# A graph-attention stack on one core: first weighing ahead of the second fold, three adds ahead of the second weighing

## What is computed

```python
for l in range(L):
    xn = _layernorm(h, ln1_g[l], ln1_b[l])
    q = (xn @ wq[l] + bq[l]).reshape(n, H, DH)
    k = (xn @ wk[l] + bk[l]).reshape(n, H, DH)
    v = (xn @ wv[l] + bv[l]).reshape(n, H, DH)
    scores = jnp.einsum('ehd,ehd->eh', q[dst], k[src]) * scale
    m = jax.ops.segment_max(scores, dst, num_segments=n)
    ex = jnp.exp(scores - m[dst])
    z = jax.ops.segment_sum(ex, dst, num_segments=n)
    attn = ex / z[dst]
    agg = jax.ops.segment_sum(attn[:, :, None] * v[src], dst, num_segments=n)
    ...
```

## Time and profile before

| | |
|---|---|
| median of 3 runs | 6146.24 us (6140.39 to 6148.77) |
| the profiled execution, its own time | 6137.13 us |
| its span, from first to last instruction | 6135.2 us |
| mean granted TensorE clock over the span | 0.759 of 2.4 GHz |
| DVE busy over the span | 3292.3 us (54%) |
| POOL busy | 3409.4 us (56%) |
| PE busy | 3529.9 us (58%) |
| first attention pass | about 3084 to 3783 us of the span |
| second attention pass | about 4181 to 4897 us |

### The profile page before, as it was taken

How to read it: one execution, slowest core, us unless ns; L and a number is a source line. 1 busy time by engine, 2 the same in 40 slices (tenths; PEclk the granted TensorE clock), 3 DMA queues, 4 the chain that set the end, 5 groups by cost and what they waited for, 6 DMA issues and landing times. The chain is left out here.

```text
span 6135.2 us, 56916 instructions
## 1 busy us (share of the span) xinstructions
PE 3529.9 (58%) x14811; PEld 2769.4 (45%) x14811; DVE 3292.3 (54%) x6546; ACT 1408.6 (23%) x3123; POOL 3409.4 (56%) x3358
## 2 busy tenths in 40 slices
PE   0365237774300067774677775887777667955551
PEld 0265126663100056663455553775555466434441
DVE  7497325555300047767678887347888742122225
ACT  0000112221200022221355553334555332200000
POOL 3778777776788747773066663005666400057771
PEclk9755656775655558876889997998999888977776
DMA  1043134443200034543277775016777610333333
GB/s 42 2 107 75 28 78 130 127 128 51 51 2 2 3 89 132 133 129 68 97 215 201 201 200 135 18 55 198 201 202 200 151 35 22 143 114 100 99 99 49
DMA packets 289802, 630.60 MB, mean 103 GB/s; under 512 B 79692, under 2 KB 134320, under 8 KB 286384
## 3 DMA queue, kind: packets, MB, share of 16 engines
q0 software_dynamic: 168256, 437.11, 29.2%
q1 hardware_dynamic: 121328, 190.89, 9.7%
HBM read 560.35 MB, written 66.48 MB: 102 GB/s over the span
## 5 line engine op out<-in xcount | busy, mean ns | idle before, releaser
L875 PE MATMUL edge_sums<-edge_rows,edge_hot 128*128 128x272 f32 (+3 forms) x4640 | 1575.3, 505 | 767.1 <-issue 285.4
L875 PEld LDWEIGHTS edge_sums<-edge_rows,edge_hot 128*128 128x128 f32 x4640 | 1155.0, 257 | 1087.6 <-issue 369.8
L809 POOL DMA_INDIRECT edge_rows<-kv_rows,dst_index x928 | 877.6, 946 | 1157.7 <-POOLq L89 661.2
L809 POOL DMA_INDIRECT edge_rows<-rel_rows,dst_other_index x464 | 471.0, 1015 | 693.3 <-ACTq L89 552.3
L809 POOL DMA_INDIRECT edge_rows<-xl_rows,dst_index x464 | 465.9, 1004 | 213.6 <-issue 135.2
L809 POOL DMA_INDIRECT edge_rows<-rows,src_index x464 | 462.2, 996 | 156.7 <-issue 131.9
L1141 PE MATMUL edge_own_rows<-dst_x,edge_hot_t 128*128 x1856 | 458.8, 392 | 37.5 <-ACT edge_hot_t L840 21.1
L211 POOL DMA_INDIRECT table_dst<-proj_dst_put_stage x350 | 417.2, 1192 | 98.0 <-issue 86.3
L1141 PEld LDWEIGHTS edge_own_rows<-dst_x,edge_hot_t 128*128 128x128 f32 x1856 | 352.3, 195 | 106.3 <-issue 53.2
L1032 DVE TENSOR_TENSOR edge_rows<-edge_rows,edge_turn_p 128x2048 f32<-128x2048 f32 x174 | 396.6, 2279 | 1.7 <-ACT edge_rows L1250 1.3
L1528 PE MATMUL proj_prod<-proj_w,proj_turned 128*128 128x512 f32 (+1 forms) x900 | 367.2, 554 | 1.0 <-ACT proj_turned L1476 0.9
(11 more groups left out here) (391 smaller groups left out, 5790.3 us busy)
## 6 DMA issues: line engine op xcount, KB each, us to landing
edge_where<-local_dst SPq DMA_DIRECT2D x174, 256.0 KB, 3.4
dst_rank_keys<-in_dst SPq DMA_DIRECT2D x85, 312.5 KB, 3.5
rel_rows<-proj_out SPq DMA_DIRECT2D x25, 1024.0 KB, 3.8
edge_where<-local_src SPq DMA_DIRECT2D x58, 256.0 KB, 3.5
edge_rows<-kv_rows,dst_index POOLq DMA_INDIRECT x928, 3.8
kv_rows<-proj_out SPq DMA_DIRECT2D x50, 260.0 KB, 2.0
edge_rows<-rows,src_index POOLq DMA_INDIRECT x464, 2.9
edge_rows<-xl_rows,dst_index POOLq DMA_INDIRECT x464, 2.9
```

The costliest lines, as they stand in the source:

```text
L809: pool.indirect_dma_start(out=self.rows[:, h * U + b, 0:self.width], out_offset=None, in_=self.source[:, :], in_offset=bass.IndirectOffset ...
L875: last = nc.tensor.matmul(sums[p % len(sums)][:, 0:width], self.hot[s % 2][:, 2 * (p % 4) + i, :], self.half(s)[:, 2 * (p % 4) + i, first: ...
```

## The change

In DVE's `step_dot`, after `multiply(4f + 3)`, the order was second fold, first weighing, fix, second weighing, four adds. It becomes first weighing, fix, second fold, three adds, second weighing, fourth add. No instruction is added or removed; nothing changes on the other engines' lists. The lines below the diff move by three.

```diff
--- before.py
+++ after.py
@@ -1069,15 +1069,18 @@
                     add(8 * d + 7, tiles[3])
                 if chunk(f):
                     multiply(4 * f + 3)
-                    fold(2 * f + 1)
                 if chunk(c):
                     weigh(2 * c)
                     tiles = e.node_tiles(nc, dve, 2 * c)
                     fix(c, tiles[0])
+                if chunk(f):
+                    fold(2 * f + 1)
+                if chunk(c):
+                    dve.wait_ge(fixed, c + 1)
+                    for n in range(3):
+                        add(8 * c + n, tiles[n])
                     weigh(2 * c + 1)
-                    dve.wait_ge(fixed, c + 1)
-                    for n in range(4):
-                        add(8 * c + n, tiles[n])
+                    add(8 * c + 3, tiles[3])
 
             def step_sum(f):
                 c, d = f - 1, f - 2
```

## The result

The changed kernel takes 6126.89 us in the median of 19 runs, the kernel before 6140.39 us in the median of as many taken beside them: a ratio of 0.9978 (95% interval 0.9972 to 0.9985), 13.5 us less. The forecast was 90 us less. Its profiled execution has a span of 6119.7 us.

What follows compares the result with a forecast made beforehand. DVE was taken to set the pace in the attention passes, waiting for slow pairs. Per pass 26 chunks x 1.8 us, less 2; two passes about 90 us, so 6146.2 - 90 = 6056 us, range 6036 to 6110.

Steps and rivals of the forecast that it cites:

- The rule named from the Trainium skill: Rival at PE's pauses: two no better than one, clock falls in each chunk, 6150 us, no change; chance 0.09.
- The end of a pass: Last chunk of each attention pass: no fold covers the pairs, last add at 7.5 instead of 5.9, 2 us lost.

Runs made afterwards that it cites:

- after_fill: The changed kernel with five idle 128x128 matmuls more per chunk on PE, behind the first half's pairs and ahead of the turn; 6052.6 us, ratio 0.986.
- after_swap: The changed kernel with expand(4f+1) put ahead of turn_scores(c) in PE's order; 6036.1 us, ratio 0.9832.
- after_work: The changed kernel with one DVE memset of 128x640 more per chunk, ahead of multiply(4f+2); 6136.9 us, ratio 1.0003.

## Why the prediction was wrong

```profile
2313.82 0.35 PE L1172 MATMUL edge_turn_p<-edge_shape,edge_lead_hot 8*128 8x8 f32 x2 [1.92 <-DVE edge_raised_t L1009]
```

From 2316.35 to 2323.10 the clock was 0.50 there, behind this pause and one of 1.12 us; a hint, if no measure for the attention passes. The runs show that in these passes pauses of 2.5 and 2.3 us ahead of the turn always or nearly always bring a fall right behind them, 2.06 and 1.85 in part of the chunks; right behind the 1.6 ahead of the pairs and the 1.4 ahead of the turn (after_fill) it came in none. The length of one pause doesn't decide it alone: in after_swap the clock fell with none above 0.8 us near, in after_work behind 1.50. A change that cuts one pause of 4.13 into 1.60 and 2.51 removes the first cause and makes a second. The rule named from the Trainium skill, "TensorE: Matmul & The Clock Gate", section "A second HAM failure mode: psum-queue depth-cycling", was on the right side: the clock fell and came back once a chunk with a pause of 2.5 us, each time costing 1.7 us.

The end of a pass was mis-sized, 6 us for 2, at least in part for the same reason: it was priced with the clock as in the rows before, and there too the pairs and the turn ran at half clock.

What stays open: why in the second pass of both profiles a few chunks (22.2 us) had no fall behind the same 2.51 us of pause, and why both kernels' losses, 1.43 and 1.70 us by different waits, end at 23.9 us a chunk. To the second the traces have more to say. In the first pass of both kernels successive falls stand 23.89 us apart in the mean, also where a chunk takes 23.7 or 24.2. A chunk that is late meets the next fall earlier in its work and loses less: behind one of 24.18 us (fall at 3610.77) the next fall came at 3634.66, 0.28 us ahead of the turn, the wait was 1.61 us instead of 1.75 and the chunk took 23.70. So the spacing of the falls seems to set the pace, and not the sum of DVE's work; what keeps that spacing isn't shown.

## What to carry to other kernels

When work is moved so that a wait on one engine goes, list the pauses of PE before and after, not only their sum: a new pause of 2 to 2.5 us at a place with no slack can cost as much as the old one of 4. Ask not only whether the clock will fall but where: the same 3.4 us at half clock cost 1.4 to 1.8 us a chunk where DVE waited for PE, and 0.1 us where it didn't. If such a pause is left, move real work of PE into it; here two exchanged statements turned 0.2% into 1.7%. An order that is right in the steady state can be wrong in the last round, where what covered the wait is missing.

## What the runs showed of the hardware

- Equal pauses don't have equal results: behind 1.85 us the clock stayed in one chunk and fell in the next. Five idle matmuls of 128x128 (1.1 us) in the pause of 2.51 us kept it at 1.00 for a stretch of 558.7 us.
- The clock can fall without a long pause near: in after_swap it did so in 10 of 25 chunks, with none above 0.8 us in the chunk since the turn.
- Successive falls stood 23.89 us apart in the mean in the first pass of both kernels, also behind a chunk of 24.18 us. Why isn't shown.
- The turn, whose weights come from a tile just written, starts 2.54 us behind the start of the instruction that releases it, the pairs 2.33 us behind theirs. Why isn't shown.
- An add that waits for the add before it on the same engine starts 0.65 us behind it; an instruction that doesn't wait starts 0.35 us behind an add.
- The same kernel took 6130 to 6140 us in most groups of runs and 6840 in one, in which DVE waited for gathers. The chip's number doesn't explain it, and the cause isn't shown.
